# Attention stage: VectorE measures the next context pair at the end of its round instead of between the round's two inverses

## What is computed

```python
x = x + _L0_xattn_ref(ctx_1024, _layernorm(x, axis=-1), L0_xattn_Wq, ...)   # here
x = x + _L0_ffn_ref(_layernorm(x, axis=-1), ...)          # mixture of experts
x = x + _L1_xattn_ref(ctx_1024, _layernorm(x, axis=-1))   # time-warping alignment
x = x + _L1_ffn_ref(_layernorm(x, axis=-1), ...)          # convolutional feed-forward
```

```python
xn = _layernorm(x, ln1_w, ln1_b)
ln = _layernorm(latents, ln2_w, ln2_b)
q = ln @ Wq
kv = jnp.concatenate([xn, ln], axis=-2) @ Wkv
k, v = jnp.split(kv, 2, axis=-1)
...
w = jax.nn.softmax(jnp.einsum('bhld,bhsd->bhls', q * scale, k * scale), axis=-1)
out = jnp.einsum('bhls,bhsd->bhld', w, v)
return out.transpose(0, 2, 1, 3).reshape(B, L, INNER) @ Wo
```

## Time and profile before

| what | us |
|---|---|
| median of 3 runs | 3253.71 (3246.82 to 3256.96) |
| the profiled execution | 3256.71 |
| its span, first to last instruction | 3255.0 |
| PE busy | 2894.3 |
| DVE busy | 2358.4 |
| POOL busy | 2007.4 |
| ACT busy | 1762.5 |

### The profile page before, as it was taken

One profiled execution on the slowest core, in us unless ns is written; L12 is line 12 of the kernel. 1 busy time (PEld: TensorE's weight loads), 2 busy tenths in 40 slices (PEclk: granted clock), 3 DMA queues, 4 the chain that ended last, 5 costly groups with the idle time before them and its releaser, 6 DMA issues. The chain is left out here.

```text
span 3255.0 us, 61553 instructions
## 1 busy us (share of the span) xinstructions
PE 2894.3 (89%) x21067; PEld 2485.9 (76%) x21070; DVE 2358.4 (72%) x5003; ACT 1762.5 (54%) x4520; POOL 2007.4 (62%) x1983
## 2 busy tenths in 40 slices
PE   6999999999999999999996999999999963078987
PEld 5888888888888888888885888888888851046765
DVE  5667676666667666766655878787877759889997
ACT  5566566656565666666563333323333326169997
POOL 5778787878787787878783333433333320058887
PEclk9999999999999999999998999999999975589999
DMA  7565555555556555565553121212121242011111
GB/s 212 109 106 103 104 106 107 106 105 107 106 110 108 106 104 109 104 107 109 104 108 109 41 66 47 73 43 74 46 70 50 59 77 50 0 34 40 46 40 40
DMA packets 704757, 272.16 MB, mean 84 GB/s; under 512 B 606168, under 2 KB 667328, under 8 KB 704448
## 3 DMA queue, kind: packets, MB, share of 16 engines
q1 hardware_dynamic: 704448, 268.23, 39.0%
HBM read 120.16 MB, written 13.73 MB: 41 GB/s over the span
## 5 line engine op out<-in xcount | busy, mean ns | idle before, releaser
L840 POOL COPY attention_probT<-attention_planesT 128x1024 uint16<-128x1024 uint16 x512 | 677.2, 1368 | 266.2 <-PE attention_turns L421 193.1
L528 ACT ACTIVATE attention_prob<-attention_turns,attention_neg_max 128x256 f32<-128x256 f32 x1024 | 468.6, 483 | 303.4 <-DVE attention_neg_max L681 302.8
L1431 POOL TENSOR_TENSOR experts_hidden_lo<-experts_weighed,experts_hidden_hi 128x512 fp32r<-128x512 f32 x192 | 255.1, 1329 | 530.9 <-ACT experts_hidden_hi L1184 530.9
L831 POOL COPY attention_planes<-attention_prob 128x1024 uint16<-128x1024 uint16 x512 | 527.1, 1060 | 20.5 <-ACT attention_prob L528 20.5
L681 DVE TENSOR_REDUCE attention_neg_max<-attention_turns 128x2 f32<-128x512 f32 x512 | 318.1, 683 | 216.0 <-PE attention_turns L406 216.0
L382 PE MATMUL attention_turns<-kv_hi,wkv 128*128 128x512 f32 x1024 | 374.6, 406 | 0.0
L1184 ACT ACTIVATE experts_hidden_hi<-experts_weighed 128x512 fp32r<-128x512 f32 x192 | 121.4, 632 | 404.3 <-DVE experts_weighed L1321 404.3
L350 PE MATMUL attention_turns<-wkv,kv_hi 128*128 128x512 f32 x1024 | 315.5, 389 | 1.9 <-ACT attention_prob L528 1.9
L421 PE MATMUL attention_turns<-attention_probT,attention_v 128*64 128x128 f32 x4096 | 253.7, 277 | 2.1 <-issue 2.1
L517 ACT COPY attention_v<-attention_turns 128x512 f32<-128x512 f32 x256 | 150.3, 589 | 187.2 <-PE attention_turns L350 187.1
L697 DVE TENSOR_TENSOR attention_turns<-attention_turns,attention_attT_lo 128x512 f32<-128x512 f32 x128 | 139.8, 1092 | 139.3 <-DMA attention_attT_lo<-inverse_rows 133.4
(11 more groups left out here) (297 smaller groups left out, 8696.7 us busy)
## 6 DMA issues: line engine op xcount, KB each, us to landing
attention_attT_lo<-inverse_rows SPq DMA_DIRECT2D x256, 128.0 KB, 2.9
experts_spread<-shares SPq DMA_DIRECT2D x256, 128.0 KB, 3.0
attention_ctx<-in_ctx SPq DMA_DIRECT2D x32, 256.0 KB, 3.0
attention_planesT<-attention_planes SPq DMA_TRANSPOSE x512, 3.2
experts_far_ctxT<-in_ctxT SPq DMA_DIRECT2D x32, 256.0 KB, 3.4
weights_ctx<-in_ctx SPq DMA_DIRECT2D x16, 512.0 KB, 3.8
out<-conv_x_out SPq DMA_DIRECT2D x15, 512.0 KB, 2.8
x_all<-in_x SPq DMA_DIRECT2D x7, 1024.0 KB, 8.9
```

Source lines behind the costliest of these rows:

```text
L528: made = act.activation(prob[n % 2][:, h, :], bank_of("s", 2 * n + e)[:, m * 256:(m + 1) * 256], ACT.Exp, bias=neg_max[:, n % 2, 2 * e + m ...
L831: pool.tensor_copy(planes[n % 2][:, g, :, :], words.rearrange("p (c b) -> p b c", b=2)).then_inc(planes_made, 1)
L840: pool.tensor_copy(words.rearrange("p (c b) -> p b c", b=2), planesT[:, g, :, :]).then_inc(joined, 1)
L1431: pool.tensor_tensor(hid_lo[n % 3][:, :], weighed[n % 2], hid_hi[n % 3][:, :].bitcast(F32), ALU.subtract).then_inc(hid_split, 1)
```

## The change

DVE's loop of rounds. In the measured i = 3 rounds both measuring steps now stand behind the last `low_k`; in round 0 they stay where they were. Nothing else differs.

```diff
                 if LAG <= u < ROUNDS + LAG:
                     scale_heads(u - LAG)
                 if u < ROUNDS:
-                    if measured is not None:
+                    if measured == 1:
                         measure_x(measured)
                     if u == ROUNDS - 2:
                         measure_first()
                     invert(n)
-                    if measured is not None:
+                    if measured == 1:
                         measure_ctx(measured)
                     if u and not i and following_pair:
                         norm_x(following_pair)
@@
                     measure_latents(following_pair)
                 if i == 1 and following_pair:
                     norm_c(following_pair)
+                if measured is not None and u:
+                    measure_x(measured)
+                    measure_ctx(measured)
                 if not u:
                     for m in range(WV, WO):
                         low_weight(m)
```

## The result

| | before | after |
|---|---|---|
| median, us | 3253.01 (3246.82 to 3256.96, 4 runs) | 3173.89 (3171.49 to 3178.66, 4 runs) |
| ratio, 95% interval | | 0.976 [0.974, 0.978] |
| profiled execution, us | 3256.71 | 3171.49 |
| its span, us | 3255.0 | 3169.8 |
| group of four rounds x 30, us | 1581.2 | 1495.4 |

Faster by 79 us between the medians, by 85 between the two profiled executions; 3168 had been forecast. All of it lies in the attention stage: the window over the same 30 groups of four rounds as in the earlier trace rows is 85.8 us shorter, and PE is busy for all but 19 us of it at a clock of 1.00.

A forecast was written before the change was run, and what follows sets the result against it. PE bounds the attention stage, losing 107.6 us there, mostly waiting for attT_lo behind VectorE's context wait. With 10.4 + 8 = 18.4 us still lost, the gain is 89: 3256.7 - 89 = 3168 us, range 3149 to 3194.

The forecast's parts named there:

- The wait and what ended it: Measured i = 3 rounds: with VectorE's context wait off the path to attT_lo, PE's 78.7 us wait goes whole.
- The bill: Attention stage: 107.6 us lost, 78.7 waiting for attT_lo, a few in restart, the rest in rounds i = 0 and 1.
- the restart: PE after its wait for attT_lo: a few us of the 107.6 lost.
- The clock: PE in i = 0 rounds: drawn-out scoring follows 2.77 us stalls, hardly any 1.9 us ones; clock goes to 1.00.
- The floor of 1473.6 us: Attention stage: 30 groups at 12.06 us for i = 3 and 0, 12.50 for i = 1 and 2; 107.6 lost above it.
- The i = 0 term: Rounds behind measured ones: ten late joins at 1.04 us each leave 10.4 us standing.
- late joins: POOL's join of planes, late in 10 of 30 measured rounds, delays the inverses' fetch and costs the next round 1.04 us.
- The i = 1 term: Late joins in 12 i = 0 rounds push i = 1 rounds by 0 to 12.5 us; 8 taken.
- Room at the end of the round: VectorE, measured rounds: context lands 10.6 to 11.7 in, statistics done 11.8 to 12.9, next maximum at 13.1; nothing charged.
- 0.2 us of cover: VectorE, worst measured round: slack between the end of measuring and the next maximum; beyond it later landings cost one for one.
- rival 3: POOL's root, waiting for statistics later than 14.3 in, holds the next joins one for one; slower, e.g. 3296 us; 2%.
- Rival 1: i = 0 rounds become VectorE's, all 1.04 us over: 31 us stay, gain 68, 3188 us; 15%.

The follow-up runs named there:

- e2: Kernel before, measuring untouched; SP issues the context's load at the start of the i = 3 round, ahead of the inverses' load: 3177.5 us, 0.977 of before.
- e9: e6 with the pair's last normalising in i = 1 rounds moved ahead of the last k split, its two small sums left behind: 3150.9 us, 0.969 of before.
- e0: The changed kernel run again without an edit, as partner of the next three runs: 3174.3 us, 0.976 of before.
- e5: Changed kernel with the context's load issued behind the transposes of the round's own planes: 3281.6 us, 1.008 of before.
- e3: Changed kernel plus the early load of the context at the start of the i = 3 round: 3177.2 us, 0.977 of before.
- e6: Changed kernel with the context's normalising in i = 0 rounds moved behind the last k split: 3158.0 us, 0.970 of before.
- e4: Changed kernel with the measuring behind attT_lo but ahead of the three k and q splits: 3237.4 us, 0.994 of before.

## Why the prediction was right

*The wait and what ended it.* Right, and shown from two sides: the weight loads' 78.7 us of waits fell to 0.4 by moving the measuring, and i = 3 rounds came down to the floor by loading earlier as well (e2). The bill took the row of the weight loads for PE's loss, though. PE's own idle time in front of the output product was 66.0 us, not 78.7. Of the 85.8 us that the stage gained, 57.4 are idle time (76.2 before, 18.8 after) and 28.4 are busy time: the same matmuls took 1505.02 us before and 1476.62 after the earlier trace rows. PE stood at the lower of its two clock levels for 44 us of this stretch before and for none of it after, worth up to 22 us. The prediction named the restart and the low clock without a size for the second; together they were a third of the gain.

*The clock.* Its going to 1.00 was right. The reading behind it was not: the prediction says that behind stalls of 1.9 us hardly any scoring is drawn out. In the trace of before, 13 of the 30 i = 0 rounds have a granted clock of 0.87 to 0.97 in their first 12 us, and 6 of these follow stalls of 1.79 to 1.95 us (0.92 behind the 1.79); 7 of the 14 rounds behind stalls of 2.0 to 2.8 us have 1.00. The length of the stall did not decide it. The sum did not hang on it.

*The floor of 1473.6 us and 107.6 lost.* Right as a bill. 21.8 us stayed lost where 18.4 had been forecast, and e9 brings all but 1.9 of them back, so the floor is real.

*The i = 0 term.* 10.4 us had been put on ten late joins of 1.04 us; the measured rounds had 11 late joins, but i = 0 rounds lost 19.5 (22.1 in e0). This is the term that was mis-sized, by 9 us. The late joins of i = 3 were right as a cause for 11 of the 16 i = 0 rounds that took over 12.6 us. In two more the fetch of the inverses was issued 1.6 and 2.0 in without a late join, and in three it was issued promptly, 0.5 in, and the data came late; the worst of these began its scaling 5.9 us after the issue and lasted 14.2 us [the fourth window above]. The 11 rounds behind a late join hold 12.5 us of the 19.5 (1.1 each, so the price per late join was right), these five 6.2. The prediction had counted late joins alone. A second miss: five of the 11 ran to between 13.4 and 13.7, above the 13.1 that it had called the most. In four of them the two normalisings of the context took 2.2 to 2.7 us instead of the 2.08 of the earlier trace rows; in the fifth the fetch was issued only 3.2 in.

*The i = 1 term.* 8 had been forecast, 1.7 to 3.2 came. Together the two are 21.2 against 18.4.

*Room at the end of the round.* Landings of 10.7 to 12.0 us in, maxima 1.04 in at all 30: right. The 0.2 us of cover was right for the round shown (0.26). e5 measures what lies beyond: rival 3 named the mechanism, and its price was too low. At the average landing of 16.7 its rule gives 3257; measured were 3281.6. It left out PE's wait for the banks and the lower clock behind it.

*Rival 1*, i = 0 rounds bound by VectorE, is half true: in 16 of 30 it cost more than 0.5 us. The margin is thinner than that: in 27 of 30 the last k split, for which they wait, ends 0.1 us before the next scores start. What fills the chain is in the traces. A normalising of 128x256 (L611) that begins while one of POOL's copies runs ends when that copy does. In the changed kernel 159 of the stage's 180 began so; 157 of these ended 0.14 to 0.16 us behind the copy and took 0.41 to 1.46 us. Of the 21 that began with POOL idle 20 took 0.39 to 0.41. bn_stats of the same width took 0.41 to 0.43 in all 149 cases beside a copy. Two i = 0 rounds of the changed kernel, u = 80 (1034) and u = 96 (1233), first in the timeline of DVE, then in that of POOL:

```profile
1034.53 0.72 DVE L611 TENSOR_SCALAR attention_ctx<-attention_ctx,attention_mean_var,attention_rstd 128x256 f32<-128x256 f32 x2
...
1233.98 2.65 DVE L611 TENSOR_SCALAR attention_ctx<-attention_ctx,attention_mean_var,attention_rstd 128x256 f32<-128x256 f32 x2
```

```profile
1034.97 2.77 POOL L843 COPY attention_probT<-attention_planesT 128x1024 uint16<-128x1024 uint16 x2 [1.32 <-DMA attention_planesT<-attention_planes]
...
1233.77 2.71 POOL L843 COPY attention_probT<-attention_planesT 128x1024 uint16<-128x1024 uint16 x2 [1.72 <-DMA attention_planesT<-attention_planes]
```

In round 96 the two normalisings end 0.15 us behind the second copy (1236.63 and 1236.48); in round 80 they began before the copies. In three rounds (24, 80, 88) the context's pair fell mostly clear of POOL, took 0.7 to 1.0 us for both, and the last k split was done 1.1 to 1.4 us early. The Trainium skill's rule ("SBUF — State Buffer", "Who interferes with whom") has the tensor_scalar normalising blocked beside POOL's copies, and the trace agrees, with the numbers above. The prediction was right that the block need not lengthen a round whose inverses are prompt (12.1 us with the same work); but those three rounds show that without it there is 1 us and more to spare for inverses that come late. No run takes POOL's copies away, so what the rounds would take without the block is not shown.

*From execution to median.* The profiled executions differ by 85 us, the medians by 79. Executions of one kernel scatter by a few us: the two traces of the changed kernel (this and e0) differ by 8.5 in span, 4.1 of it in the groups and 4.8 behind round 123, less 0.5 ahead of them. That the forecast lies within 6 us of the median owes something to this scatter, and to terms that missed both ways: i = 0 by 9 too low, i = 1 by 5 to 6 too high.

## What to carry to other kernels

On an in-order engine ask of each wait what is queued behind it and which engine needs that first: here the wait for one and the same transfer cost a round 2.8 us between the inverses, 2.3 ahead of the three splits, and nothing behind these 2 us of work. Before moving the work, look at who issues the transfer: one line in SP's order did the same. Once the wait is gone, sum the stage against the round that has none of the extra work; the rest of that bill named the next two moves, which gave 23 us more.

## What the runs showed that was not expected

Instruction fetches disturb data: where a 16 KB packet of queue q8, about 1 us long, starts while DMA transposes are in flight, the first of the two transposes that the join needs lands 4.7 us after its issue instead of 3.2, and POOL's join waits 1.7 us instead of 0.2 (medians of the changed kernel). This held for 26 of 26 late joins of the changed kernel and 22 of 22 with the code shifted by 96 PE instructions. In e0 to e3, e6, its repetition and e9 it held for 163 of 167, and none of the 119 rounds was prompt with such a packet; in e4 and e5, with their other delays, many joins were late without one (11 of 30 and 31 of 46). Which engine's instructions q8 brings was not tried apart; that its packets moved with PE's count speaks for PE. Why such a packet of 1.0 us delays a transpose by 1.5 stays open.
